# A two-layer transformer on one core: the bias on scores moved inside each sorting step, the finish's weights loaded in the last layer, VectorE in GpSimd's place in the last chunk of the latents

## What is computed

```python
scores = jnp.einsum('blhe,bshe->bhls', queries, keys)
A = sparsemax(scale * scores)      # sorts the 32 scores of each head and token
out = jnp.einsum('bhls,bshd->blhd', A, values)
out = jnp.transpose(out, (0, 2, 1, 3)).reshape(B, L, H * D)
return out @ Wo + bo
```

## Time and profile before

| | us |
|---|---|
| median of 3 runs | 2086.99 |
| lowest and highest of them | 2086.12, 2088.26 |
| the profiled execution: its own time | 2092.38 |
| the profiled execution: its span | 2090.7 |
| TensorE, VectorE busy in the span | 1944.8, 1603.9 |
| ScalarE, GpSimd busy in the span | 1042.1, 426.6 |

### The profile page before, as it was taken

How to read it: one execution, slowest core, us unless ns; L and a number is a source line. 1 busy time by engine, 2 the same in 40 slices (tenths; PEclk the granted TensorE clock), 3 DMA queues, 4 the chain that set the end, 5 groups by cost and what they waited for, 6 DMA issues and landing times. The chain is left out here.

```text
span 2090.7 us, 35235 instructions
## 1 busy us (share of the span) xinstructions
PE 1944.8 (93%) x11938; PEld 1199.9 (57%) x11938; DVE 1603.9 (77%) x3816; ACT 1042.1 (50%) x2239; POOL 426.6 (20%) x862
## 2 busy tenths in 40 slices
PE   6869999999999999999989999998888999999998
PEld 3433333333333333333269999997766777777776
DVE  6778998888888888888356555554888999999983
ACT  3426667777677777777855555554521112222112
POOL 4654123322222222222212212221000000000000
PEclk9978999999999999999999999999989999999998
DMA  5555301111111111110112232214610000000005
GB/s 198 180 174 165 126 28 50 50 40 63 65 63 46 65 64 65 65 64 12 52 62 84 84 113 81 86 52 152 197 41 21 12 10 21 21 21 21 11 11 166
DMA packets 112984, 151.57 MB, mean 72 GB/s; under 512 B 13092, under 2 KB 95662, under 8 KB 112432
## 3 DMA queue, kind: packets, MB, share of 16 engines
q1 hardware_dynamic: 96384, 107.73, 16.0%
q0 software_dynamic: 13344, 40.16, 5.6%
q10 hardware_dynamic: 3088, 1.58, 0.4%
HBM read 85.82 MB, written 65.31 MB: 72 GB/s over the span
## 5 line engine op out<-in xcount | busy, mean ns | idle before, releaser
L882 ACT ACTIVATE at_wt<-at_B 128x512 f32<-128x512 f32 (+3 forms) x1280 | 607.3, 538 | 250.6 <-PE at_B L981 234.1
L1285 DVE TENSOR_REDUCE at_piece_max<-at_A 128x1 f32<-128x512 f32 x768 | 488.7, 682 | 65.5 <-PE at_A L962 62.8
L999 PE MATMUL at_O<-at_wt,at_v 128*32 128x512 f32 (+3 forms) x2560 | 313.2, 542 | 0.0
L1282 DVE CUSTOM_DVE_ANT_0 at_junk<-at_A,s_hide 128x128 bf16<-128x128 f32 (+3 forms) x512 | 230.1, 487 | 68.8 <-PE at_A L962 68.4
L774 POOL TENSOR_SCALAR_AFFINE_SELECT at_wt<-at_wt 128x128 f32<-128x128 f32 x512 | 147.8, 294 | 606.3 <-ACT at_wt L882 597.3
L1506 PE MATMUL ex_H<-ex_xT,ex_w_in 128*128 128x256 f32 x1920 | 248.5, 286 | 4.4 <-DVE ex_xT L1615 4.4
L1506 PEld LDWEIGHTS ex_H<-ex_xT,ex_w_in 128*128 128x128 f32 x1920 | 237.6, 193 | 4.7 <-DVE ex_w_out L1640 4.7
L2259 ACT ACTIVATE l_act_g<-l_G 128x512 f32<-128x512 f32 x80 | 47.9, 599 | 306.1 <-PE l_G L2173 241.8
L962 PE MATMUL at_A<-s_k,s_q 96*128 96x512 bf16 (+2 forms) x480 | 165.7, 363 | 22.0 <-PEq L105 9.7
L1654 DVE TENSOR_TENSOR ex_h<-ex_act_a,ex_H 128x256 f32<-128x256 f32 x160 | 66.8, 417 | 145.8 <-ACT ex_act_a L1561 145.1
L981 PE MATMUL at_B<-s_q,s_k 99*128 99x512 bf16 x480 | 160.3, 352 | 5.9 <-ACT at_wt L882 4.9
(11 more groups left out here) (290 smaller groups left out, 2925.4 us busy)
## 6 DMA issues: line engine op xcount, KB each, us to landing
buf<-at_room POOLq DMA_DIRECT2D x10, 1040.0 KB, 11.0
s_first_rows<-buf SPq DMA_DIRECT2D x40, 260.0 KB, 2.7
expert_out<-at_room POOLq DMA_DIRECT2D x8, 1024.0 KB, 5.0
s_raw_in<-in_W_in SPq DMA_DIRECT2D x8, 1024.0 KB
mx_ye<-expert_out SPq DMA_DIRECT2D x32, 256.0 KB, 3.7
q_parts<-parts SPq DMA_DIRECT2D x16, 384.0 KB, 3.5
s_down<-in_x SPq DMA_DIRECT2D x8, 512.0 KB, 4.6
xn<-s_raw_in SPq DMA_DIRECT2D x8, 512.0 KB, 5.6
```

Source lines behind the costliest of these rows:

```text
L882: act.activation(wt[(HP * p + h) % NE_][:, q0:CH], pB_of(p, h, u)[:, q0:CH], ACT.Exp, scale=D ** -0.5).then_inc(wt_ready, 1)
L999: pe.matmul(pO[j % 2][rows, q0:CH], vs[n % 3][:, kt // TPC, kt % TPC, :], wt[(HP * p + h) % NE_][:, q0:CH], start=kt < 2 and not late, sto ...
L1282: ins = dve.tensor_tensor_reduce(junk[(HP * i + h) % 4][:, 0:w], pA[slot % NA][:, 0:w], hide[:, CH - w:CH], 1.0, NEG, ALU.add, ALU.max, ac ...
L1285: ins = dve.tensor_reduce(top, pA[slot % NA][:, 0:w], AX.X, ALU.max)
```

## The change

- In `layer1`, `keep_scores` stands behind the first sorting or threshold item of each of the steps 6 to 9.
- `Wo` gets a place that is kept from before `layer1` (`s["wo"]`); SyncE loads it at the start of `layer1`, on the semaphore of that stage's constants, for which VectorE waits once before it casts `seg`. In the finish the load is gone, and with it TensorE's wait; VectorE's `add` counts one load less on `part_in[0]`.
- In the last chunk of `latents`, `turned` and `left` of pairs 1 and 2 run on VectorE instead of GpSimd, and its order there is: products, turned 1, turned 2, low 0, values, left 1, left 2, low 1, low 2.

```diff
--- before.py
+++ after.py
@@ -270,10 +270,11 @@
             for c in range(NCH):
                 turned(c, 0)
                 left(c, 0)
-                turned(c, 1)
-                turned(c, 2)
-                left(c, 1)
-                left(c, 2)
+                if c + 1 < NCH:
+                    turned(c, 1)
+                    turned(c, 2)
+                    left(c, 1)
+                    left(c, 2)
 
         @block.scalar
         def _(act):
@@ -433,6 +434,19 @@
                 dve.tensor_tensor(parts[k][c % 2][0:rows_of(k), 2], rest[k][0:rows_of(k)], parts[k][c % 2][0:rows_of(k), 1],
                                   ALU.subtract).then_inc(low_ready, 1)
 
+            def turned(c, k):
+                dve.wait_ge(pair_used, 2 * (PAIRS * c + k) + 2)
+                dve.wait_ge(high_ready, PAIRS * (c - 1) + k + 1)
+                rows = rows_of(k)
+                dve.tensor_tensor(rot[k][0:rows], by_cos[k][0:rows], by_sin[k][0:rows], ALU.add).then_inc(rot_ready, 1)
+
+            def left(c, k):
+                dve.wait_ge(high_ready, PAIRS * c + k + 1)
+                dve.wait_ge(low_ready, PAIRS * (c - 1) + k + 1)
+                rows = rows_of(k)
+                dve.tensor_tensor(rest[k][0:rows], rot[k][0:rows], parts[k][c % 2][0:rows, 0],
+                                  ALU.subtract).then_inc(rest_ready, 1)
+
             def values(c):
                 dve.wait_ge(vl_made, c + 1)
                 wait(dve, v_out[c % 2], 16 * (c // 2))
@@ -449,10 +463,17 @@
                 products(c, 2)
                 if ahead:
                     variances(c + 2)
+                if c + 1 == NCH:
+                    dve.wait_ge(high_ready, PAIRS * c + 1)
+                    turned(c, 1)
+                    turned(c, 2)
                 low(c, 0)
                 values(c)
                 if ahead:
                     normalise(c + 2)
+                if c + 1 == NCH:
+                    left(c, 1)
+                    left(c, 2)
                 low(c, 1)
                 low(c, 2)
 
@@ -2105,6 +2126,7 @@
             sp.dma_start(iota[:], d["c_iota"]).then_inc(iota_in, 16)
             sp.dma_start(z[1][:].rearrange("p t n -> p (t n)"), d["c_seg"]).then_inc(consts_in, 16)
             sp.dma_start(inv_k[:], d["c_inv_k"]).then_inc(consts_in, 16)
+            sp.dma_start(s["wo"][:], d["Wo"].rearrange("(k p) n -> p k n", p=P)).then_inc(consts_in, 16)
 
             def load(c):
                 wait(sp, stored[c % 2], 16 * (c // 2))
@@ -2432,7 +2454,7 @@
             for t in range(1, TPC):
                 keep_scores(0, t)
             shares()
-            dve.wait_ge(consts_in, 32)
+            dve.wait_ge(consts_in, 48)
             dve.tensor_copy(seg[:], z[1][:].rearrange("p t (n w) -> p (t n) w", w=2)[:, :, 0]).then_inc(ones_ready, 1)
             dve.wait_ge(ones_ready, 2)
             for c in range(NCH):
@@ -2442,21 +2464,18 @@
                         means()
                     scored_next = c + 1 < NCH and SCORE <= i < SCORE + TPC
                     for n, item in enumerate(items_of(i)):
-                        if item == SORTS and scored_next:
-                            keep_scores(c + 1, i - SCORE)
-                            scored_next = False
                         if item < SORTS:
                             sort(c, item)
                         else:
                             threshold(c, item - SORTS)
+                        if scored_next and n == 0:
+                            keep_scores(c + 1, i - SCORE)
                         if i == 0 and n == 0 and c:
                             result(c - 1)
                     if c + 1 < NCH and i in SCORE_LOWS:
                         score_lows(c + 1, SCORE_LOWS.index(i))
                     if c + 1 < NCH and i == LOW:
                         low(c + 1)
-                    if scored_next:
-                        keep_scores(c + 1, i - SCORE)
             result(NCH - 1)
 
 
@@ -2473,7 +2492,7 @@
             return ctx.enter_context(nc.semaphore("fi_" + name))
 
         ident = s["ident"]
-        wo = sb("wo", [P, EC, E])
+        wo = s["wo"]
         head = [sb(f"head{u}", [P, 2, E]) for u in range(2)]
         part = [sb(f"part{u}", [P, 2, E]) for u in range(2)]
         hT = [sb(f"hT{u}", [P, EC, 2 * P]) for u in range(2)]
@@ -2503,8 +2522,6 @@
 
         @block.sync
         def _(sp):
-            sp.dma_start(wo[:], d["Wo"].rearrange("(k p) n -> p k n", p=P)).then_inc(part_in[0], 16)
-
             def store(t, u):
                 sp.wait_ge(res_ready, t + 1)
                 sp.dma_start(one(out_rows, t), res[u][:]).then_inc(stored[u], 16)
@@ -2522,8 +2539,6 @@
 
         @block.tensor
         def _(pe):
-            pe.wait_ge(part_in[0], 32)
-
             def turn(t, u):
                 pe.wait_ge(head_ready, t + 1)
                 wait(pe, hT_ready, t - 1)
@@ -2575,7 +2590,7 @@
 
             def add(t, u):
                 dve.wait_ge(o_made, t + 1)
-                dve.wait_ge(part_in[u], 16 * (t // 2 + 2 - u))
+                dve.wait_ge(part_in[u], 16 * (t // 2 + 1))
                 wait(dve, stored[u], 16 * (t // 2))
                 dve.tensor_tensor(res[u][:], pO[u][:], part[u][:], ALU.add).then_inc(res_ready, 1)
 
@@ -2647,6 +2662,7 @@
         mixing(nc, d, s)
         keep("mixed_first", [P, TILES // B, E])
         s["mixed"] = (s["mixed_first"], normal_rows(s)[:, 0:TILES // B])
+        keep("wo", [P, EC, E])
         layer1(nc, d, s)
         finish(nc, d, s)
```

## The result

| us | before | changed |
|---|---|---|
| median of 4 runs each, same chip | 2087.62 | 2058.78 |
| lowest, highest | 2086.12, 2092.73 | 2056.16, 2061.19 |
| profiled execution: own time, span | 2092.38, 2090.7 | 2056.16, 2054.4 |

The ratio is 0.9852, with an interval of 0.9834 to 0.9871: 30.9 us faster (28.8 between the medians), where 28.5 were forecast. The time, 2058.78, is 0.3 us from the predicted one. So each stage is compared by itself here.

What follows compares the result with a forecast made beforehand. In layer 1 TensorE (59.5 us a chunk) and VectorE (58.1) make each other late through one PSUM tile `Z`. -1.3 - 7.1 - 16.7 - 3.4 = -28.5 us, from the median of 2086.99 to 2058.5; range 2054 to 2067.

Steps and rivals of the forecast that it cites:

- latents: Last chunk of `latents`: four operations on VectorE instead of GpSimd bring the last store earlier, -1.3 us, bounds 0 and -2.5.
- chunk 0: First chunk of layer 1: 1.9 of a 5.45 us TensorE wait stay, a 1.00 wait goes; -7.1 us, between 2.9 and 9.0.
- chunks 1 to 6: Steady chunks of layer 1: both TensorE waits for `keep_scores` go, 6 x 2.79 = -16.7 us.
- finish: Finish: `Wo` loaded early and only the addition waits for partial rows; -3.4 us, between -0.4 and -4.6.
- 62.25 - 2.79 = 59.5: Steady chunk of layer 1: period less two idle waits, taken as TensorE's own work and the new period, 59.5 us.
- VectorE's own work: Steady chunk of layer 1: 62.25 - 1.17 - 2.95 = 58.1 us, with TensorE longer by 1.4 us.
- the second rival: Layer 1: VectorE becomes the bound of the chunks; half of 16.7 lost gives 2067, all 2075; chance 12%.
- I take the clock as held: Chunk 0: TensorE stays at 2.4 GHz after the remaining 1.9 us wait, worth 1.26 + 1.28 us more.
- the first rival: Clock falls after chunk 0's remaining wait (3 us lost) and rises one projection late in the finish (1.5): 2063; chance 15%.
- the lower term: Chunk 0: by the skill's rule that bursts after waits start cold, the sum is 3 us smaller.
- the rule of exclusion: Last chunk of `latents`: VectorE operations with two SBUF inputs and GpSimd ones reading SBUF exclude each other; gain near 0.
- The third rival: Finish: bound by its rows from the start, so it gains only 0.4 us: 2061.5; chance 5%.

Runs made afterwards that it cites:

- the experiment with one wait back: The changed kernel with the bias addition of step 6 alone back behind all four items of its step: 2065.27 us, 0.9937 of the kernel before.
- the kernel in which the wait itself was gone: The changed kernel with the bias addition of step 6 in chunk 0 put ahead of `hidden`: 2046.22 us, 0.9843 of the kernel before.

## Why the prediction was right

| part | forecast | measured |
|---|---|---|
| latents | -1.3 | -1.5 in the trace, -1.1 by time alone |
| chunk 0 | -7.1 | -5.7 |
| chunks 1 to 6 | -16.7 | -19.8 (373.33 - 353.54, the six periods added) |
| finish | -3.4 | -3.8 in this pair of traces, -3.3 by the means of all traces and by time alone |
| sum | -28.5 | -30.8 in the trace, -30.9 by the ratio, -28.8 between medians |

**The waits of a steady chunk** went as argued: none is left for `Z`, VectorE has no wait for it, the slack held when 1.1 us of it was taken, and what is late next is TensorE's own work. The size was off. "Chunks 1 to 6 with a period of 59.5 us" was 58.93. The step that was mis-sized is `62.25 - 2.79 = 59.5` as TensorE's own work: a wait costs 0.26 us more than its idle time, as the experiment with one wait back showed (1.61 for 1.35). With that, the term is 6 x 3.3. (The prediction has four additions changing places in a chunk; by its own walk and in the code they are three, since the one of step 9 stays where it was.)

**VectorE's own work** was put at 58.1 and a lead of 1.4. It is 58.93 - 1.13 = 57.8. The same items take 0.3 less, since the bias now stands between two that depend on each other: the row at 1634.47 to the one at 1636.20, with the bias between, is 1.73, where an item (1.25) and a bias (0.60) would be 1.85. Steps 7 and 8 each have such a place, which makes 0.2 of the 0.3. This was the argument against the second rival ("the bias, between two dependent items, gives the first time to finish"), and had no term of its own. As TensorE is the bound, it brought nothing in time.

**Chunk 0** had the right remaining wait, 1.9 forecast and 1.94 measured, and the wrong clock: "I take the clock as held" was the step that failed. `down` took 3.24 us where 1.89 stands at full speed, and the scores 2.02 for 1.67, as the first rival had it. It cost less than the 3 us of that rival. Part by part, against the earlier trace rows: 3.51 from the wait, 1.00 and its 0.26, 0.91 from faster scores and nothing from `down`: 5.7, the 5.66 measured. The prediction held that the matmuls would have to lose 3 us before TensorE is as late as VectorE; they lost 1.7 (1.35 and 0.35), and with that TensorE was the later one by 0.85, VectorE's idle time before chunk 1. Holding the clock would have brought about 1 us in chunk 0 and up to 1 in chunk 1, an estimate from the kernel in which the wait itself was gone, since VectorE is the bound close behind; a bound that the prediction looked for in the steady chunks and not there. The Trainium skill (TensorE: Matmul & The Clock Gate, HAM oscillation) says that bursts with waits between them start cold again, in an example with longer waits. By it I should have taken the lower term, and here the trace agrees with it, at 1.94 us; at 1.35 and 1.44 it does not, in twelve waits before and in those of the experiment above.

**The latents** came as walked, with undisturbed prices on VectorE. The overlap with GpSimd did not arise: its last subtraction ends at 107.91 + 1.16 = 109.07, where `turned` starts at 109.06. So the rule of exclusion that was weighed there was not put to the test by the change. Two rows of the trace of before bear on it:

```profile
111.46 1.08 DVE L433 TENSOR_TENSOR parts<-rest,parts 128x512 bf16<-128x512 f32 x1 [0.61 <-ACT parts L300]
111.96 1.70 POOL L256 TENSOR_TENSOR rot<-by_cos,by_sin 64x512 f32<-64x512 f32 x1
```

VectorE's `low(0)` started 0.54 us before GpSimd's `turned` of pair 1 ended (110.74 + 1.26) and took 1.08 us, not 0.68; GpSimd's `turned` of pair 2 started 0.58 us before that one ended and took 1.70 us, where the shortest of its kind takes 1.26. Each lost 0.4 us of an overlap of 0.5 to 0.6, which fits waiting out most of the other.

**The finish** came as argued. The first transpose is 0.5 us behind the first load, as forecast, and the projection took 3.09 us, not 3.54. When the clock rises there varies with the execution (2.92 to 3.73 us for that projection over all traces), not with the change. The third rival (a gain of 0.4, bound by its rows) is false. The wait of VectorE for 48 in layer 1 cost nothing that shows: the start of chunk 0 behind `l_ones` is 18.2 us in the changed trace and 19.1 before, and 18.2 too with the bias alone, which has no such load.

The sum was nearer than its terms: chunks 1 to 6 brought 3.1 more, latents and finish 0.6 more, chunk 0 1.4 less; and the medians are 2 us closer together than the ratio has it.

## What to carry to other kernels

When an engine takes its queue in order, put the short step that frees a single buffer where its input is just ready and somebody still has slack, here between two dependent long ones; with slack on both sides it then costs nothing to be a place off. When you size a wait of TensorE from its idle column, add the weight load and the overlap that it lays bare: 0.26 us for each wait here, a fifth of it. Judge such an edit by the period of the loop in the trace: steady periods repeat within 0.1 us across chips, while whole executions of one kernel spread over up to 9 us, and chips differ by 9.

The best versions run are those with the bias ahead in chunk 0 alone, ahead everywhere, or with the scalings on ScalarE too: 0.9843, 0.9842 and 0.9841 against 0.9855. These intervals overlap; the periods of chunks 0 to 2 say 2.0, 2.0 and 2.9 us better than the change.

## What the runs showed that was not expected

**The same wait is followed by either speed of TensorE, by the execution.** Before the last `down` of chunk 7 TensorE waits 2.03 or 2.04 us in every kernel. In the earlier trace rows its eight matmuls then take 3.05 us; in the changed kernel

```profile
1998.17 1.99 PE L2216 MATMUL l_D<-s_down,l_h 128*128 128x256 f32 x8 [2.04 <-DVE l_h L2371]
```

and with the latents' part alone, whose layer 1 is that of before:

```profile
2013.70 3.06 PE L2215 MATMUL l_D<-s_down,l_h 128*128 128x256 f32 x8 [2.04 <-DVE l_h L2370]
```

Over the traces the eight matmuls take 1.99 or 2.00 us in seven, 2.41 to 2.73 in four, and 3.05 or 3.06 in two, with no tie to the order of the code: the kernel with the bias alone has 2.73 and the changed one on two chips 1.99 and 2.70. Nor does the clock hold for good in the seven: the turns and small products that follow have short waits between them, and before the finish the granted clock is 0.50 in all thirteen traces. What differs is when it falls. In the changed kernel's first trace it is 1.00 for 8 us behind the wait, in its second 0.50 from 2 us behind it on (a row from each):

```profile
1998.17:2006.17 8.00, 5.75 (x36) 4.48 (x36) 3.39 (x3) 2.54 (x5) 0.00 (x0) 1.00 0.19 66
1991.76:2007.76 16.00, 12.06 (x51) 9.96 (x50) 2.00 (x5) 3.88 (x8) 0.00 (x0) 0.50 0.09 33
```

The stretch from the last `hidden` to the finish is 14.4 to 15.9 us long in the seven, 16.5 and 16.6 in the two with the slowest `down` (there the clock came back for some 4 us in between, to 0.90 and more), and 17.9 to 18.2 in the four. That is 1.8 of the 36.2 between the two profiled executions. In chunks 0 to 6, waits of 5.45 and 3.06 us were followed by slow matmuls, those of 1.46 and less never, and the ones of 1.91 to 1.94 in chunk 0 in all four traces that have them (`down` 2.89 to 3.24 us behind them). What decides at 2 us was not tried and stays open; a forecast that rests on a wait of that length should carry both values.

**A chip's time is not the program's.** The first chip takes 9 us longer for the kernel before than three others, yet its steady periods in layer 1 are theirs to 0.1 us. The 9 us lie in attention: from the first to the last product into `at_O` it is 930.2 and 929.0 us in the two traces of the first chip, and 916.7 to 921.0 in the eleven of the others. Why attention is slower there stays open.
